# A one-core adaLN block (SSM mixer and mixture of experts): bias rows on twelve partitions, a later load of two Toeplitz groups, and a new order of the routing with ScalarE's one-hots

## The reference, cut to what matters

```python
h = layernorm(x) * (1 + ca) + sa
x = x + ga * attn(h)                       # attn: see below
h = layernorm(x) * (1 + cb) + sb
x = x + gb * ffn(h)

def attn(x):                               # a state-space mixer
    xz = layernorm(x) * ln_g + ln_b  @ in_w.T + in_b
    x_proj, z = halves of xz
    y = causal_convolution(x_proj, kernel(A_log, B, C, log_dt))    # length 1024
    y = (y * silu(z)) @ out_w.T + out_b
    return clip(y + residual, -10, 10)

def ffn(x):                                # top-1 mixture of 8 experts, N = 4096 tokens
    x_flat = x @ W_proj + b_proj
    expert = argmax(x_flat @ W_gate)       # weight of the only expert is 1
    # each expert takes its first 1024 tokens, in token order
    h = gelu(layernorm(tok @ W1[e] + b1[e]) * ln1_g[e] + ln1_b[e])
    out = h @ W2[e] + b2[e]                # scattered back to the tokens
    return layernorm(outputs) * ln_g + ln_b
```

## Time and profile before

| | us |
|---|---|
| median of 3 runs | 308.73 (308.03 to 310.51) |
| the profiled execution | 312.26 |
| its span, first to last instruction | 309.8 |
| busy: TensorE, VectorE, GpSimd, ScalarE | 261.5, 230.5, 189.0, 143.7 |
| mean granted TensorE clock | 0.955 |

### The profile page before, as it was taken

One profiled execution on the slowest core, in us unless ns is written; L12 is line 12 of the kernel. 1 busy time (PEld: TensorE's weight loads), 2 busy tenths in 40 slices (PEclk: granted clock), 3 DMA queues, 4 the chain that ended last, 5 costly groups with the idle time before them and its releaser, 6 DMA issues.

```text
span 309.8 us, 6445 instructions
## 1 busy us (share of the span) xinstructions
PE 261.5 (84%) x1759; PEld 169.3 (55%) x1760; DVE 230.5 (74%) x896; ACT 143.7 (46%) x364; POOL 189.0 (61%) x225
## 2 busy tenths in 40 slices
PE   0998887979937999876769999999999999999740
PEld 0646545779915677642423556566556565566430
DVE  1799987989992999889923587777677777777730
ACT  3578565665201377820100655454554554454520
POOL 2589898201910366610544668888888888887461
PEclk9999999999985999997995999999999999999995
DMA  6930299956089947771013123223222223221000
GB/s 145 216 136 1 59 272 286 249 129 151 2 285 259 283 126 206 203 228 44 2 54 99 51 61 93 77 61 93 76 68 85 79 64 90 75 68 46 26 6 0
DMA packets 47279, 35.29 MB, mean 114 GB/s; under 512 B 4557, under 2 KB 42555, under 8 KB 47128
## 3 DMA queue, kind: packets, MB, share of 16 engines
q1 hardware_dynamic: 42278, 24.70, 28.8%
q0 software_dynamic: 3744, 9.77, 10.8%
q10 hardware_dynamic: 1234, 0.53, 0.8%
HBM read 24.34 MB, written 11.08 MB: 114 GB/s over the span
## 4 chain that ended last, share of the span: by engine, by line
PE 57%; DVE 21%; POOL 8%; issue 5%; DMA 3%; ACT 1%; SPq 1%; POOLq 0%; ACTq 0%; DVEq 0%
PE PS L1500 13%; PE PS L1483 12%; PE PS L1491 7%; PE PS L1485 4%; POOL rs L508 4%; PE PS L1473 3%; DVE Z L1012 2%; PE PS L1390 2%; PE PS L1386 2%; DVE SBk L390 2%; DMA CP<-in_L_attn_C_param_dram 2%; PE PS L1502 2%; PE PS L1326 2%; DVE st L863 2%; PE PS L1339 2%
## 5 line engine op out<-in xcount | busy, mean ns | idle before, releaser
L803 ACT ACTIVATE V<-PS,gb1T 128x128 f32<-128x128 f32 x156 | 58.6, 456 | 59.5 <-PE PS L1491 58.2
L1500 PE MATMUL PS<-BIG,V 128*128 x312 | 47.2, 291 | 3.4 <-DVE Wst L1203 1.8
L611 POOL DMA_INDIRECT SBk<-rows,idgi x39 | 41.8, 1072 | 12.9 <-issue 7.7
L1500 PEld LDWEIGHTS PS<-BIG,V 128*128 128x128 f32 x312 | 43.4, 196 | 6.3 <-issue 4.5
L619 POOL DMA_INDIRECT out_dram<-Wst,idsi x39 | 39.7, 1017 | 11.1 <-DVE Wst L1214 7.3
L1197 DVE TENSOR_SCALAR V<-PS,mv,rs 128x512 f32<-128x512 f32 x39 | 31.4, 806 | 17.8 <-POOL rs L629 17.3
L1483 PE MATMUL PS<-BIG,V 128*128 x78 | 42.9, 634 | 1.6 <-issue 1.6
L629 POOL TENSOR_TENSOR rs<-ve,half 128x2 f32<-128x2 f32 x42 | 30.5, 726 | 14.5 <-DVE ve L1218 13.7
L1187 DVE BATCH_NORM_STATS2 st<-PS 128x6 f32<-128x512 f32 x39 | 27.1, 695 | 11.9 <-PE PS L1485 11.5
L1491 PE MATMUL PS<-ident,V 128*128 128x128 f32 x156 | 25.5, 286 | 0.0
L583 POOL TENSOR_TENSOR rs<-ve,half 128x4 f32<-128x4 f32 x8 | 8.1, 1017 | 25.8 <-DVE ve L1036 25.8
(11 more groups left out here) (252 smaller groups left out, 545.5 us busy)
## 6 DMA issues: line engine op xcount, KB each, us to landing
BIG<-k_pad SPq DMA_DIRECT2D x32, 256.0 KB, 5.6
X<-in_L_attn_x_dram SPq DMA_DIRECT2D x4, 512.0 KB, 6.8
BIG<-in_L_ffn_W_dram SPq DMA_DIRECT2D x1, 2048.0 KB, 9.3
rows<-GL SPq DMA_DIRECT2D x4, 512.0 KB, 4.5
rows<-Hh SPq DMA_DIRECT2D x8, 256.0 KB, 3.7
out_dram<-Hh SPq DMA_DIRECT2D x8, 256.0 KB, 3.7
rows<-U SPq DMA_DIRECT2D x4, 512.0 KB, 3.2
Wst<-la_rows SPq DMA_DIRECT2D x1, 1024.0 KB, 4.6
```

The lines of the kernel that those rows point to most:

```text
L611: pool.indirect_dma_start(out=XG[:, u, :], out_offset=None, in_=rows, in_offset=bass.IndirectOffsetOnAxis(ap=idgi[:, t:t + 1], axis=0), bo ...
L803: a.activation(AT[:, u, k, :], PS[:, 3, P * k:P * k + P], ACT.Gelu, bias=gb1T[:, 1, bass.ds(e, 1), k], scale=gb1T[:, 0, bass.ds(e, 1), k]) ...
L1500: m.matmul(dst, AT[:, u, k, :], W2s[:, bass.ds(e, 1), k, :].rearrange("p a d -> p (a d)"), start=(k == 0), stop=False)
```

## The change

Three things are changed together.

**1. Bias rows on twelve partitions.** The shift is copied three times side by side (`shift3`, 128 x 12), so one matmul gives a 12 x 136 result: partition 4m + b holds part m's copy of batch row b. One ScalarE copy takes it out. The addition and the five steps of the split work on 12 x 136. They now stand in VectorE's stream between the two halves of the chunk recurrence. The spreading matmul takes all twelve rows with a selector `rowsel` (12 partitions, 4 x 128 columns, bf16) in place of `ones3`; GpSimd writes it with a memset and three `affine_select` instructions, after the zeroing of the states.

**2. Later load.** SyncE waits for `s_in` 6 ahead of both of the last two Toeplitz groups.

**3. Routing.** ScalarE copies a unit's logits ahead of its tokens, with a semaphore of their own (`s_lg`). VectorE assigns tiles 0 to 23 ahead of the last unit's norm, and TensorE counts them ahead of that unit's transposes. ScalarE makes the row one-hots of tiles 0 to 15: sixteen `Square` of (column - row) and two `Relu` of (1 - square). VectorE makes those of tiles 16 to 23 and 24 to 31. The row numbers are computed ahead of the tile experts.

```diff
@@ sync
             for k in range(TRING, 8):
-                sp.wait_ge(s_in, k - TRING + 1)
+                sp.wait_ge(s_in, TRING)
                 toeplitz(k)
@@ gpsimd
             g.memset(one8[:], 1.0)
+            step.mark(g.memset(rowsel[:], 0.0))
             for k in range(2):
                 step.mark(g.memset(seg[k][:], 1.0))
             step.settle()
+            for n in range(3):
+                last = g.affine_select(out=rowsel[:], in_=rowsel[:], pattern=[[-1, B], [0, P]],
+                                       compare_op=ALU.not_equal, fill=1.0, base=-B * n, channel_multiplier=1)
+                if n < 2:
+                    step.mark(last)
+                    step.settle()
+            last.then_inc(s_sel, 1)
@@ scalar
             act.wait_ge(s_r2, 1)
-            a.copy(row_pb[:, 0:(B - 1) * PJ], PS[0:3, 1, 64:64 + (B - 1) * PJ])
-            a.copy(row_pb[:, (B - 1) * PJ:], pb_product(B - 1)).then_inc(s_r2c, 1)
+            a.copy(row_pb[:], PS[0:3 * B, 1, 0:PJ]).then_inc(s_r2c, 1)
...
-                a.copy(XF[:, HT * q:HT * q + HT, :], src[:, :, 0:D])
-                a.copy(LG[:, HT * q:HT * q + HT, :], src[:, :, D:PJ]).then_inc(s_pje, 1)
+                a.copy(LG[:, HT * q:HT * q + HT, :], src[:, :, D:PJ]).then_inc(s_lg, 1)
+                a.copy(XF[:, HT * q:HT * q + HT, :], src[:, :, 0:D]).then_inc(s_pje, 1)
...
+            act.wait_ge(s_rown, 1)
+            for c4 in range(ACT_OHC):
+                for t in range(OHC * c4, OHC * c4 + OHC):
+                    last = a.activation(OR[:, t], iota_b[:], ACT.Square, bias=rown[:, t:t + 1])
+                last.then_inc(s_far, 1)
+            for c4 in range(ACT_OHC):
+                act.wait_ge(s_far, c4 + 1)
+                near = OR[:, OHC * c4:OHC * c4 + OHC]
+                a.activation(near, near, ACT.Relu, bias=one8[:, 0:1], scale=-1.0).then_inc(s_oh, 1)
@@ vector
+                if c2 == 0:
                     dve.wait_ge(s_r2c, 1)
-                    step.mark(v.tensor_tensor(row_pb[:].rearrange("p (b e) -> p b e", b=B),
-                                              row_pb[:].rearrange("p (b e) -> p b e", b=B),
-                                              bc(row_pj[:].unsqueeze(1), [3, B, PJ]), ALU.add))
+                    step.mark(v.tensor_tensor(row_pb[:], row_pb[:], row_pj[:], ALU.add))
                     step.settle()
                     three_parts(row_pb[:], part_pb[:], part_pb[:]).then_inc(s_r2e, 1)
...
-            normed_here(2 * B - 1)
...
-                dve.wait_ge(s_pje, (a + n) // HT)
+                dve.wait_ge(s_lg, (a + n) // HT)
...
+                if k == 0:
+                    v.tensor_scalar(rown[:, rng], rowi[:, rng], -1.0, None, ALU.mult).then_inc(s_rown, 1)
...
             assign(0)
+            normed_here(2 * B - 1)
             running_counts(0)
             places(0)
+            assign(1)
             dve.wait_ge(s_row, 1)
-            row_onehots(0).then_inc(s_oh, 1)
-            assign(1)
-            row_onehots(1).then_inc(s_oh, 1)
+            row_onehots(ACT_OHC).then_inc(s_ohd, 1)
             running_counts(1)
@@ tensor
-            for b in range(B):
-                last = m.matmul(pb_product(b), bc(cbsT[:, 0, b:b + 1], [P, 3]), WPG[:], start=True, stop=True)
-            last.then_inc(s_r2, 1)
+            m.matmul(PS[0:3 * B, 1, 0:PJ], shift3[:], WPG[:], start=True,
+                     stop=True).then_inc(s_r2, 1)
...
+                if k == 1:
+                    pe.wait_ge(s_pje, 2 * B)
...
+                if n == 2 * B - 1:
+                    counts(0)
                 if early:
                     rows_turn2(n)
                 if n >= 1:
                     project(n - 1)
                 if 0 <= n < 2 * B and not early:
                     rows_turn2(n)
-                if n == 2 * B - 1:
-                    counts(0)
```

76 lines of the change are left out of this document (43 added, 33 removed).

## The result

The changed kernel takes 299.5 us (median of 4 runs, 297.96 to 300.67); the kernel before, run beside it, takes 309.62 (308.03 to 312.57). The ratio is 0.966 with a 95% interval of 0.9565 to 0.9754, so the change is worth 10.1 us, 3.3%. The forecast was 295.7 with a range of 292.0 to 300.5: faster, as said, inside the range, but near its slow end; 13.0 us had been worked out. In what follows a ratio compares fast runs alone (a run over 1.5% above the fastest of its kernel counts as slow), while a median takes all runs.

The account below looks back on a forecast made before the run. Before the expert stage the chain was taken to pass through VectorE twice, at the convolution's end and in the routing; 4.7 + 2.3 + 4.9 + 1.5 - 0.4 = 13.0 us off 308.73 gave 295.7, range 292.0 to 300.5.

Parts of the forecast that it names:

- The hold of 1.5 us: Near 55.5 us, GpSimd's selector writes hold VectorE, which loses 1.5 us (0 up to 3.6).
- (c): Rival at the selector: GpSimd doesn't hold VectorE, as a 12-partition write is short; 294.2 us, chance 0.12.
- (b): Rival: GpSimd holds VectorE 3.6 us and TensorE drops to 1.2 GHz in the dense products; 299.8 us, chance 0.12.
- (f): Rival: stage 2 isn't shortened, because gate products wait for banks anyway; 301.6 us, chance 0.05.
- (d): Rival: the two late Toeplitz groups arrive late, the eighth 3 us behind its need; 298.2 us, chance 0.07.
- (e): Rival in the routing: ScalarE's Squares cost much more than 0.41 us; slower, 311.9 us at 1.5 each, chance 0.03.
- Part 5: After the row numbers: VectorE's tile experts lie beside GpSimd's first gather, costing 0.4 us (0 to 1).
- gain 4.7: End of the convolution: the gated turning starts at 90.3 instead of 95.05 us.
- I take 3.4: Routing: the early assignment and one one-hot fewer bring the second running counts 3.4 us sooner after the mixer units.
- (a): Rival: the granted clock falls again ahead of the experts; 297.2 us, chance 0.15.
- Parts 4 and 5: First experts: the clock stays up, gaining 1.5 us (0 to 2.2); tile experts beside the gather take off 0.4.
- I count nothing: Later load: TensorE's 1.71 us issue stall at 67.72 may go, but bank 0's products wait for VectorE's states; no gain.

Follow-up runs that it names:

- s_early_blk: Whole change with the selector built at the kernel's start and the bias block behind both halves of the recurrence; 304.58 us, ratio 0.9851.
- p1_bias: Kernel before with only the bias rows on twelve partitions, their new place and the selector; 303.6 us, ratio 0.979.
- r_fill: Whole change plus two unread TensorE matmuls ahead of the first running counts; 297.19 us, ratio 0.9599.
- b_fill: Kernel before with eight instead of six unread matmuls behind the token matmul; 308.92 us, ratio 1.0008.
- a_oldload: Whole change without the later load of the Toeplitz groups; 299.91 us, ratio 0.9687.
- r_noact: Whole change with all row one-hots on VectorE; 299.43 us, ratio 0.9651.
- r_oldorder: Whole change with the old order: last norm ahead of the assignment, running counts behind the projection; 298.7 us, ratio 0.9658.
- s_early: Whole change with the selector built at the kernel's start; 297.83 us, ratio 0.9579.
- p2_load: Kernel before with only the later load of the Toeplitz groups; 306.21 us, ratio 0.9857.
- p3_route: Kernel before with only the routing changed; 307.52 us, ratio 0.9946.

## Why the prediction was right or wrong

**Right, and shown.**

- *The hold of 1.5 us*: recurrence at 66.46 against 65.00 with the selector moved away. The Trainium skill ("SBUF — State Buffer", "SBUF: two separate sides") has the pair of ports shared with GpSimd as an exclusive lock: a VectorE instruction in a 2-port mode, or with two inputs in SBUF, and a GpSimd instruction hold it against each other for a whole instruction. The traces agree: three steps in s_early_blk end within 0.2 us of the end of a GpSimd piece each, and the selector's instructions count (0.73 us and more for 0.43) though they touch twelve partitions. So rivals (c), no hold, and the hold of (b), 3.6 us, are out.
- *The block*: 1.8 us for 1.7, and p1_bias puts the first unit at 93.03.
- *Bank 2* at 79.11 for 79.1, *gate products* starting at 78.09 for 78.1.
- *The rest of the convolution, where the clock holds*: in r_fill the last bank is done at 88.42 for 88.45 and the gated turning starts at 90.13 for 90.3.
- *The gated turning and what follows, at full clock*: 2.88 us instead of 5.42, a gain of 2.5 for 2.3 (about 1.6 against the 4.5 of the other traces of before's code). Rival (f) is out.
- *The late groups* (d): no wait for them in the change as made.
- *ScalarE* (e): 0.30 us for a Square, 0.41 forecast; it decides nothing.
- *Which wait is last at the token matmul*: GpSimd's plane.
- *From token matmul to row numbers*: 1.40 us (147.47 to 148.87) instead of 2.59, a gain of 1.2 for 1.0.
- *Part 5*: from the row numbers to the first expert product it is 5.86 us, 6.00 before, so nothing of the 0.4 that was taken off shows, and no run has it alone.

**Wrong: "gain 4.7" up to the gated turning, measured 3.2.** The step that failed is that everything from bank 2 on would be 2.1 us late and nothing more. Behind 2.45 us of waiting TensorE was at 1.2 GHz between 79 and 83 us, and the last bank was done at 90.11, not 88.45. The gate products came with breaks and ended at 91.76, not near 89.7. That was the second half of rival (b), which I had tied to a hold of 3.6 us ("idle before bank 2 for over 3 us"); it happened at 2.45 with a hold of 1.5, in two of four executions of the same code. Price 1.7 us, for 2 estimated.

**Wrong: "I take 3.4" for the running counts, measured 0.46.** This is the mis-sized term that decides the result: the routing gave 2.3 us instead of 4.9. Up to the end of the first 24 tiles' places VectorE gained 1.3 us (13.19 us after the last unit's start before, 11.93 after). The assignment did escape GpSimd's write (0.36 us a step for 1.32), but the scan that is now beside that write takes 1.52 us instead of 0.56, so 1.0 of it came back; and the assignment waits 0.43 us for its logits. Then the one-hot taken away (1.14 us from start to start) made room for a wait of 1.88. I followed VectorE's queue and not what its new order does to TensorE: the norm of the last tiles is what TensorE waits for, and I had moved it behind five assignment steps. r_fill shows that 2 us of it are the clock.

**Wrong in size: the clock at the first experts.** It stayed up, as forecast (against rival (a)), and in the profiled pair this stretch gained 3.0 us for the 1.1 of Parts 4 and 5 together. The forecast took one profile of before for all of its executions. By the three traces of its routing (b_fill, above) the fall costs it 3.0, 1.6 and 0 us, and b_fill's median doesn't move.

**Wrong: Part 2 "I count nothing".** For the whole change the medians agree (a_oldload), but alone it gives 3.8 us, of which the link over GpSimd explains 1.2 in the trace. The reason that I gave, bank 0's products wait for VectorE's states, is not what hides it; in the kernel before the stall moved GpSimd's output bias and through it VectorE, and the new place of the block cuts this link.

The sum by the profiles is 5.8 + 0.1 + 2.3 + 3.0 = 11.1, and 1.1 behind it that isn't the change's; by the medians 10.1 for 13.0. That the profiled pair differs by 12.2, close to 13.0, is luck: the 1.5 and 2.6 us that the convolution and the routing fell short are mostly made up by 1.9 more than forecast at the first experts and by the 1.1 behind, and both come from the one execution of before that was profiled. The two new falls of the clock, priced at 1.7 and 2 us, are enough for the 3 us between forecast and medians, though the first doesn't come in every execution.

## What to carry to other kernels

When an instruction is moved out of one collision, look for which instruction takes its place beside the other engine's write, and ask what the engine downstream now waits for: here VectorE's saved time came back as TensorE's low clock and from there as VectorE's own wait. Parts of a change that remove waits on the same path don't add: measure each alone and each taken out of the whole. Where a forecast rests on one profile, compare the stretches that the change doesn't touch with a second one before adding up. Where an engine holds another for whole instructions, the place of a small instruction is worth more than its width, 0.22 us against 2.3 here.

## What the runs showed of the hardware

**The clock's fall varies between executions.** The whole change, r_noact, r_fill and r_oldorder have the same code up to 120 us, wait for bank 2 for 2.45 or 2.46 us and turn it at 79.11, 79.00, 79.04 and 79.03. In the first two the clock was 0.50 from 80 to 82 us and the first unit starts at 94.69 and 94.60; in the other two it stayed at 1.00, and the unit starts at 93.01 and 93.00. s_early fell there behind a wait of 1.97 us. A term that rests on such a fall is a chance, not a number, and one profile can't price it.

**A stall that ends with an instruction packet.** TensorE loses time to "issue" at about 68 us, between two rows of short products: 0.53 us in the change as made, 0.34 in p2_load and at most 0.82 in the other kernels with the later load, but 1.71, 1.98, 2.20, 3.01 and 3.34 in before, p3_route, p1_bias, a_oldload and b_fill, which load the seventh Toeplitz group beside it. The DMA share from 66 to 68 us is 0.86 in a_oldload and 0.04 in the change as made. The traces also have the packets of a queue q8 of the kind "instruction", 16 KB each. In us:

| trace | stall | q8's packet | TensorE goes on |
|---|---|---|---|
| p2_load | 0.34 | 65.62 to 66.56 | 67.97 |
| the change as made | 0.53 | 66.14 to 67.42 | 68.76 |
| before | 1.71 | 67.10 to 68.14 | 69.43 |
| a_oldload | 3.01 | 69.00 to 69.99 | 71.29 |
| b_fill | 3.34 | 68.88 to 69.83 | 71.29 |

In all fourteen traces TensorE goes on 1.2 to 1.5 us after this packet has ended, and the packet starts at 65.6 to 66.4 us with the later load, at 67.1 to 69.0 beside the seventh group. So the stall is long where the packet is late, and it is late only beside that load. That TensorE's next instructions are in it, and what delays it, is concluded from these times and not shown.

**An unread matmul can be worth more than it costs.** The two matmuls of r_fill (1.88 us, in a wait of 1.5) took 2.3 us off the median of the whole change and 2.1 off that of s_early (297.83 to 295.69). The intervals of the ratios overlap in both pairs; the marks of the traces, 1.6 us in the routing in each pair, say the same.
